# Layer 1's feed-forward scales the second projection's input instead of its output, and small weights are fetched a stage earlier

## What is computed

```python
x = x + tanh(g_xattn[l]) * attention_l(layernorm(x), ctx_1024, ...)
x = x + tanh(g_ffn[l])   * feed_forward_l(layernorm(x), ...)
```

```python
h = gelu(x @ w1[e]) * (x @ v1[e])            # for each expert e
out = sum_e gate[token, e] * (h @ w2[e]) + bias
```

## Time and profile before

| what | value |
|---|---|
| three timed executions | 1097.5, 1100.67, 1102.53 us, median 1100.67 |
| the profiled execution | 1095.08 us, of which the profile's span is 1093.3 us |
| mean granted clock of PE | 0.913 of full speed |
| busy share of the span | PE 80%, DVE 68%, ACT 52%, POOL 38% |
| set-up, then layer 0 (attention, feed-forward) | begin at 0, 16.68 and 118.91 us |
| layer 1 (attention, feed-forward) | begin at 181.65 and 423.34 us |
| layer 2 (attention, feed-forward) | begin at 702.27 and 813.53 us |
| layer 3 (attention, feed-forward) | begin at 873.81 and 1002.59 us |

### The profile page before, as it was taken

How to read it: one execution, slowest core, us unless ns; L and a number is a source line. 1 busy time by engine, 2 the same in 40 slices (tenths; PEclk the granted TensorE clock), 3 DMA queues, 4 the chain that set the end, 5 groups by cost and what they waited for, 6 DMA issues and landing times. The chain is left out here.

```text
span 1093.3 us, 17068 instructions
## 1 busy us (share of the span) xinstructions
PE 879.5 (80%) x5336; PEld 666.8 (61%) x5336; DVE 746.9 (68%) x1844; ACT 565.1 (52%) x1091; POOL 414.0 (38%) x559
## 2 busy tenths in 40 slices
PE   1899585789999994888888888489966668995795
PEld 0677463666666653666666666368854437995573
DVE  3699577589999984666757656468856514555786
ACT  1587263367777772545646454257743333432364
POOL 1543214133344431565656656444311042321143
PEclk9899688679999996999999999789988889998699
DMA  4000000000000001000000000000000020000001
GB/s 129 9 2 2 1 0 24 1 21 21 22 22 21 22 21 39 1 1 1 1 1 1 1 1 1 2 2 2 2 22 1 0 77 1 1 2 1 0 1 39
DMA packets 25926, 14.13 MB, mean 13 GB/s; under 512 B 11095, under 2 KB 25326, under 8 KB 25710
## 3 DMA queue, kind: packets, MB, share of 16 engines
q1 hardware_dynamic: 25838, 13.04, 4.4%
HBM read 11.99 MB, written 1.05 MB: 12 GB/s over the span
## 5 line engine op out<-in xcount | busy, mean ns | idle before, releaser
L1495 POOL TENSOR_TENSOR L1f_h<-L1f_h,L1f_gb 128x512 f32<-128x512 f32 (+1 forms) x96 | 152.2, 1588 | 104.6 <-DVE L1f_h L1788 96.2
L762 ACT ACTIVATE L_pt<-bank 128x512 f32<-128x512 f32 x224 | 127.0, 597 | 40.7 <-PE bank L637 26.6
L423 POOL TENSOR_TENSOR L_kc<-L_kc_all,const 128x256 fp32r<-128x256 f32 x96 | 58.8, 616 | 154.7 <-PE bank L637 73.6
L1624 ACT ACTIVATE L1f_a<-bank 128x512 f32<-128x512 f32 (+1 forms) x96 | 57.3, 596 | 111.8 <-PE bank L1549 111.8
L1788 DVE TENSOR_TENSOR L1f_h<-L1f_a,bank 128x512 f32<-128x512 f32 (+1 forms) x96 | 65.5, 682 | 70.2 <-ACT L1f_a L1624 69.6
L1796 DVE TENSOR_TENSOR L1f_h_lo<-L1f_h,L1f_h_hi 128x512 fp32r<-128x512 f32 (+1 forms) x96 | 88.0, 917 | 11.1 <-ACT L1f_h_hi L1637 11.1
L892 DVE TENSOR_REDUCE L_ms<-bank 128x2 f32<-128x512 f32 x128 | 83.6, 684 | 4.1 <-PE bank L595 3.5
L749 ACT ACTIVATE L_part<-bank,L_bias_ca,const 128x256 fp32r<-128x256 f32 x128 | 68.7, 562 | 29.5 <-PE bank L572 28.5
L1547 PE MATMUL bank<-L1f_xt_hi,big_hi 128*128 128x512 f32 (+1 forms) x192 | 77.5, 403 | 0.1
L1549 PE MATMUL bank<-L1f_xt_hi,big_lo 128*128 128x512 f32 (+1 forms) x192 | 76.5, 398 | 0.0
L1548 PE MATMUL bank<-L1f_xt_lo,big_hi 128*128 128x512 f32 (+1 forms) x192 | 76.3, 397 | 0.0
(11 more groups left out here) (410 smaller groups left out, 2505.0 us busy)
## 6 DMA issues: line engine op xcount, KB each, us to landing
L_raw<-in_L_ffn_w_dram SPq DMA_DIRECT2D x8, 176.0 KB, 2.3
L_raw<-in_L_ffn_v_dram SPq DMA_DIRECT2D x8, 176.0 KB, 2.5
const<-in_const_dram SPq DMA_DIRECT2D x1, 1036.0 KB
x<-in_x_dram SPq DMA_DIRECT2D x2, 512.0 KB
L_raw<-in_L_ffn_w_dram SPq DMA_DIRECT2D x8, 128.0 KB, 2.6
mask<-in_mask_Bx1xSxS_ff_dram SPq DMA_DIRECT2D x2, 512.0 KB
out_dram<-x SPq DMA_DIRECT2D x2, 512.0 KB
L_raw<-in_L_ffn_w_dram SPq DMA_DIRECT2D x8, 48.0 KB, 2.4
```

The lines of the kernel that those rows point to most:

```text
L762: act.activation(pt[:, g // 2, (g % 2) * NS + (HEADS_1[i] if own_keys else i)], b_st[(g * NS + i) % 2][:], ACT.Exp, scale=scale).then_inc( ...
L1495: pool.tensor_tensor(h[0:m, r], h[0:m, r], gb[0:m, gate_slot(c)], ALU.mult).then_inc(sem["h_done"], 1)
```

## The change

**Layer 1's feed-forward** is a function of its own, `ffn_gated_input`. Once per expert PE spreads the gates (`gate`), DVE multiplies the raw input by them into `xg_raw`, ACT casts `xg_hi`, POOL subtracts to `xg_lo` (both are `gated`), and the second projection (`u`) works on these. `up` is cut into `g` (first projection) and `u`, and `g` stands five chunks ahead of `u`; the tile `a` has 7 buffers instead of 4. POOL's multiplication of `h` and ACT's copy `gb` are gone; `split` follows one chunk behind. The front of the next batch stands at other chunks, its choice of experts in five parts over five chunks.

**Transfers**: the bias vectors of both attentions are issued in set-up, those of layer 0 ahead of the attention weights, those of layer 2 behind them. The integer weights of layer 2's feed-forward and the five loads of layer 3's attention are issued at the start of layer 2's attention. **Layer 2's feed-forward**: the three low parts are made behind the first scaling. **Layer 3's attention**: the eight value products leave the preparation and stand in the loop, one per sequence (`context_values`), through the bank that the transposes use.

```diff
+                def load_bias(layer):
+                    names = {0: ("L0_xattn_bq", "L0_xattn_bkv"), 2: ("L2_xattn_bq", "L2_xattn_bk")}[layer]
+                    for i, name in enumerate(names):
+                        for t in range(4):
+                            sp.dma_start(pr.bias_t[layer][NG * i:NG * i + NG].rearrange("g (h t d) -> g h t d", h=GH, t=4)[:, :, t],
+                                         ins[name][0:D].rearrange("(g h d) -> g h d", g=NG, h=GH)).then_inc(pr.bias_in[layer], 16)
+
+                load_bias(0)
...
+                load_bias(2)
...
-    ("values", 1), ("proj", 1, 1), ("pv", 0, 0), ("sums", 0), ("scores", 1, 0), ("scores", 1, 1), ("parts", 0), ("y", -1), ("keys", 2, 0),
+    ("context_values", 1), ("values", 1), ("proj", 1, 1), ("pv", 0, 0), ("sums", 0), ("scores", 1, 0), ("scores", 1, 1), ("parts", 0), ("y", -1), ("keys", 2, 0),
...
+                if layer == 2:
+                    for dst, src in ((pr.wi[:, 0:3], ins["L2_ffn_w_gate"].rearrange("(c p) d -> p c d", p=P)),
+                                     (pr.wi[:, 3:6], ins["L2_ffn_w_up"].rearrange("(c p) d -> p c d", p=P)),
+                                     (pr.wi[:, 6:9], ins["L2_ffn_w_down"].rearrange("d (c p) -> d c p", p=P))):
+                        sp.dma_start(dst, src).then_inc(pr.wi_in, 16)
+                    for dst, src in ((pr.w3[:, 1], ins["L3_xattn_Wk"]), (pr.w3[:, 0], ins["L3_xattn_Wq"]), (pr.w3[:, 2], ins["L3_xattn_Wv"]),
+                                     (pr.w3[:, 3].rearrange("p (c n) -> p c n", n=D), ins["L3_xattn_Wo"].rearrange("(c p) n -> p c n", p=P)),
+                                     (pr.bo3[:], ins["L3_xattn_bo"].partition_broadcast(P))):
+                        sp.dma_start(dst, src).then_inc(pr.w3_in, 16)
                 if layer == 0:
...
-                for e in range(B):
-                    bank = pr.bank[(NC + e) % 8]
-                    if e >= 4:
-                        pe.wait_ge(sem["prep_act"], e - 4 + 1)
-                    pe.matmul(bank[:], pr.ctx_t2[:, e].rearrange("p a s -> p (a s)"), wv[:], start=True, stop=True).then_inc(sem["prep_pe"], 1)
-                pe.wait_ge(sem["prep_act"], 12)
+                pe.wait_ge(sem["prep_act"], 4)
...
+                def context_values(b):
+                    pe.wait_ge(sem["xt_lo"], b + 1)
+                    pe.matmul(b_turn[:], pr.ctx_t2[:, b].rearrange("p a s -> p (a s)"), wv[:], start=True, stop=True).then_inc(sem["v_done"], 1)
...
+                def context_values(b):
+                    act.wait_ge(sem["v_done"], b + 1)
+                    act.copy(v_all[:, b], b_turn[:]).then_inc(sem["v_taken"], 1)
...
+                    if layer == 2 and i == 0:
+                        low_weights()
+
+                def low_weights():
+                    for m in range(3):
+                        cols = slice(m * 384, (m + 1) * 384)
+                        dve.wait_ge(sem["prep_act"], m + 1)
+                        prep(dve.tensor_tensor(lo[:, cols], pr.bank[m][:, 0:384], hi[:, cols].bitcast(F32), ALU.subtract))
 
...
+def ffn_gated_input(pr):
+    nc, ins = pr.nc, pr.ins
+    n = "L1f"
+    C, E, K = 24, E1, K1
+    N, NQ = NI * C, NI * E
+    AHEAD = 5
+    RA, R = 7, 4
+    LAG = 3
...
+            run(("moments", 0), ("prepare", 0), ("scale", 0), ("moments", 1), ("turn", 0), ("moments", 2), ("logits", 0))
+            run(*[("route", (0, part)) for part in range(5)])
+            run(("g", 0), ("g", 1), ("moments", 3), ("g", 2), ("gates", 0), ("g", 3), ("gate", 0), ("gated", 0), ("g", 4))
+            for k in range(N):
+                i, c = divmod(k, C)
+                if k + AHEAD < N:
+                    run(("g", k + AHEAD))
+                run(("u", k), ("mul", k))
+                if c % 3 == 0 and k // 3 + 1 < NQ:
+                    run(("gate", k // 3 + 1))
+                if c % 3 == 1 and k // 3 + 1 < NQ:
+                    run(("gated", k // 3 + 1))
+                if k >= 1:
+                    run(("split", k - 1))
+                if k >= LAG:
+                    run(("down", k - LAG))
+                if c == LAG - 1 and i:
+                    run(("y_copy", i - 1))
+                if i + 1 < NI:
+                    if c == 4:
+                        run(("scale", i + 1))
+                    if c == 6:
+                        run(("turn", i + 1))
+                    if c == 8:
+                        run(("logits", i + 1))
+                    if 9 <= c < 14:
+                        run(("route", (i + 1, c - 9)))
+                    if c == 15:
+                        run(("gates", i + 1))
+                if i and c == 11:
+                    run(("y_turn", i - 1))
+            run(("split", N - 1))
+            run(*[("down", k) for k in range(N - LAG, N)])
+            run(("y_copy", NI - 1), ("y_turn", NI - 1))
+
+        with nc.Block() as block:
+            @block.sync
+            def _(sp):
+                sp.dma_start(router[:], ins["L1_ffn_router_w"]).then_inc(sem["loaded"], 16)
...
+                def gated(q):
+                    pool.wait_ge(sem["xg_hi"], q + 1)
+                    need(pool, sem["u_done"], 3 * (q - 1))
+                    pool.tensor_tensor(xg_lo[:, q % 2], xg_raw[:, q % 2], xg_hi[:, q % 2].bitcast(F32), ALU.subtract).then_inc(sem["xg_lo"], 1)
...
+                def g(k):
+                    i = k // C
+                    pe.wait_ge(sem["xt_lo"], i + 1)
+                    need(pe, sem["act_done"], k - 1)
+                    product(b_g[k % 2], weights_at(k)[0], rows(k), xt_hi[:, i % 2], xt_lo[:, i % 2]).then_inc(sem["g_done"], 1)
+
+                def gate(q):
+                    i, e = divmod(q, E)
+                    pe.wait_ge(sem["gts_ready"], i + 1)
+                    need(pe, sem["xg_raw"], q - 1)
+                    pe.matmul(b_gate[q % 2][:], sel[:, e:e + 1].to_broadcast([P, P]), gts[:, i % 2], start=True, stop=True).then_inc(sem["gate_done"], 1)
+
+                def u(k):
+                    q = k // 3
+                    pe.wait_ge(sem["xg_lo"], q + 1)
+                    need(pe, sem["h_done"], k - 1)
+                    product(b_u[k % 2], weights_at(k)[1], rows(k), xg_hi[:, q % 2], xg_lo[:, q % 2]).then_inc(sem["u_done"], 1)
...
+                def g(k):
+                    m = rows(k)
+                    act.wait_ge(sem["g_done"], k + 1)
+                    need(act, sem["h_done"], k + 1 - RA)
+                    act.activation(a[0:m, k % RA], b_g[k % 2][0:m], ACT.Gelu).then_inc(sem["act_done"], 1)
+
+                def gated(q):
+                    act.wait_ge(sem["xg_raw"], q + 1)
+                    need(act, sem["u_done"], 3 * (q - 1))
+                    act.copy(xg_hi[:, q % 2], xg_raw[:, q % 2]).then_inc(sem["xg_hi"], 1)
+
...
+                def gate(q):
+                    dve.wait_ge(sem["xt_raw"], q // E + 1)
+                    dve.wait_ge(sem["gate_done"], q + 1)
+                    need(dve, sem["xg_lo"], q - 1)
+                    dve.tensor_tensor(xg_raw[:, q % 2], xt_raw[:, q // E % 2], b_gate[q % 2][:], ALU.mult).then_inc(sem["xg_raw"], 1)
+
+                def mul(k):
+                    m, r = rows(k), k % R
+                    dve.wait_ge(sem["act_done"], k + 1)
+                    dve.wait_ge(sem["u_done"], k + 1)
+                    need(dve, sem["lo_done"], k + 1 - R)
+                    dve.tensor_tensor(h[0:m, r], a[0:m, k % RA], b_u[k % 2][0:m], ALU.mult).then_inc(sem["h_done"], 1)
+
...
         with nc.sbuf_tensor("mask2", [P, NT, 2, S2], F32) as pr.mask2:
-            ffn(pr, 1)
-            attention(pr, 2, own_keys=False, masked=True, biased=True, scale=D ** -0.5)
-        ffn(pr, 2)
-        attention3(pr)
+            ffn_gated_input(pr)
+            with nc.sbuf_tensor("wi", [P, 9, P], I32) as pr.wi, nc.sbuf_tensor("w3", [P, 4, 512], F32) as pr.w3, \
+                    nc.sbuf_tensor("bo3", [P, D], F32) as pr.bo3:
+                attention(pr, 2, own_keys=False, masked=True, biased=True, scale=D ** -0.5)
+                ffn(pr, 2)
```

301 lines of the change are left out of this document (260 added, 41 removed).

## The result

The changed kernel takes 1048.5 us, the median of four runs (1046.1 to 1051.8), against 1100.9 us (1097.5 to 1102.5, four runs) for the kernel before: a ratio of 0.952, 95% interval 0.948 to 0.956. The forecast was 1046 us. In its profiled execution the span is 1048.7 us instead of 1093.3, with nearly the same mean clock of PE (0.916 against 0.913).

A forecast was written before the change was run, and what follows sets the result against it. The chain of `h` through POOL, not the matmuls, bounds layer 1's feed-forward. Terms -40.0 - 4.7 - 4.0 - 7.2 + 1.6 = -54.3 us give 1040.8 from the profiled 1095.08, 1046 from the 1100.67 median; range 1034 to 1070.

The forecast's parts named there:

- Layer 1's feed-forward: Layer 1's feed-forward: PE's matmuls alone remain, with 5 us allowed for all stops; 212.5 us from 252.52, -40.0 us.
- ring: Layer 1's feed-forward: making the gated input, gates' matmul through POOL's subtraction, takes 4.3 to 4.7 us against 5.8.
- the entry: Layer 1's feed-forward, before the first `down`: costs the same as before, within 2 us either way.
- Two signs: Layer 1's feed-forward, new profile: 6.5 to 6.7 us from expert to expert, and no PE wait for `h_lo`.
- The account of the stop: Layer 1's feed-forward, old kernel: PE loses 1.26 us per expert; `h_lo` is late as DVE's subtraction waits for POOL.
- Layer 2's attention: Entry of layer 2's attention: without the wait for bias vectors, token transposes start earlier; -4.7 us, between -3.5 and -5.
- feed-forward (-4.0; -4.0): Layer 2's feed-forward: DVE's 2.63 us wait for `wi` goes, first product comes earlier; -4.0 us, -3.6 to -4.2.
- Layer 3's attention: Layer 3's attention: early loads give -14.2 us, value products in the loop cost +7.0; -7.2 us, between -14 and 0.
- The entry (-14.2; -13.7): Layer 3's attention: first token transposes come 6.9 us after the block's start instead of 21.1, -14.2 us.
- stand several steps after the product: Layer 3's attention loop: POOL's `values` and PE's `y` await the value copy several steps after the product, 0.9 + 0.6 us.
- Set-up: Set-up: sixteen bias transfers keep SP issuing until 23.4, first attention begins near 24.0; +1.6 us, between +0.5 and +3.
- the slower case: Layer 1's feed-forward: PE's in-order wait for `xg_lo` blocks ready work, an expert takes 9.2 us; 1127 us, 3%.

The follow-up runs named there:

- gated_only: The kernel before with only layer 1's feed-forward replaced by the changed kernel's `ffn_gated_input`: 1065.6 us, ratio 0.968.
- att3_pieces: The changed kernel with POOL's 128x1920 subtraction in layer 3's attention cut into five of 128x384: 1042.1 us, ratio 0.949.
- best2: The changed kernel with layer 2's bias transfers and eight attention weights of layers 1 and 2 issued later, POOL's layer 3 subtraction in five pieces: 1034.7 us, ratio 0.940.
- pool_extra: The changed kernel with one more POOL multiplication of spare tiles per chunk of layer 1's feed-forward, its result unused: 1108.0 us, ratio 1.007.
- ahead0: The changed kernel with no `g` running ahead in layer 1's feed-forward, each directly before its own `u`: 1054.1 us, ratio 0.952.

## Why the prediction was right, step by step

- **Layer 1's feed-forward (-40.0; -39.9, and -40.2 in `gated_only`).** Right in mechanism and size. Expert 6.46 us, ring 4.29 us against 4.3 to 4.7, 1.47 us to spare against 1.1, stops of a few us. Inside the sum two terms missed and nearly cancelled: the stretch behind the first `down` was 210.0 instead of 212.5 us, and the entry 24.6 instead of 21.8 us, outside the 2 us that I had allowed. Both have one main reason: I let 26 matmuls stand ahead of the first `down`, but with `g` five ahead there are 42, and 16 by 0.231 is 3.7 us. Two signs came out only in part: experts beside a batch's front took up to 7.8 us, not 6.7, and PE still waited three times for `h_lo`, 0.6 us in all. The account of the stop was right in its chain and one-sided in its cause: I read the collision of the earlier trace rows as what made `h_lo` late, but the collisions are as many as before and cost nothing now; the chain was too long for its lag. So the gates' place was not the only cure: the new order with one more chunk of lag gives 32 of the 40 us.
- **Layer 2's attention (-4.7; -4.9) and feed-forward (-4.0; -4.0).** Right. The waits were the bound, and what stood next was where the rows put it. In twelve executions with these parts the two blocks took 160.8 to 165.4 us, in two without them 171.3 and 171.5. How the 4.0 us of the feed-forward divide between the early load and the later low parts was not tested.
- **Layer 3's attention (-7.2; -3.7 in that execution).** The entry (-14.2; -13.7) and the iteration (+0.88; +0.85) were right. The step that failed was the sentence that the waits for the value copy "stand several steps after the product". In the first iteration POOL's product for the values now waits 2.5 us for it, and its cast and subtraction of the next block's weights, which stand behind, come to lie on DVE's copy: a stop of 4.01 us instead of 2.05, and 7.6 us at a mean clock of 0.55 instead of 0.78. `att3_pieces` shows that the stop is a cause (117.85 us against 123.0 to 125.1 in nine profiles with the uncut instruction); how much of the lost clock follows from it stays open, since `best2` with the same pieces took 121.71. That the block's size was still as forecast on the mean is in part luck: 123.9 us over nine executions with the unaltered changed code, 131.0 over two of before, -7.1.
- **Set-up (+1.6; +2.4, over ten executions with this set-up +1.9 to +3.6).** The mechanism was right (SP's queue sets the end; begin 24.36 against 24.0), the size low: the wait for the weights' spreading ended at 25.81, not 25.4, and behind it DVE reached `xn` 2.0 us later than before.
- **The untouched blocks.** The forecast had no term for them, and they moved: +4.3 and +1.6 us. `gated_only` shows that layer 1's attention moves by more than that with nothing ahead of it changed.
- **The whole.** Sum in the profile -44.6 instead of -54.3 us; the timed medians -52.3. The difference of 9.7 is +4.3 and +1.6 of the untouched blocks, 3.5 of layer 3's attention and 0.8 of set-up, less 0.5 of the rest. The forecast misses by 2 us in the medians and by 9.7 in the profiles, because the profiled execution of before lies 5.8 us under its median and that of after 1.9 us above. That 1046 lies so near 1048.5 is therefore partly luck: single executions of one kernel differ by more.

The rivals: the slower case did not come, and nothing in the changed kernel is near it. But `pool_extra` took the time to 1108 us largely by its mechanism, the wait for `xg_lo` ahead of ready work (34.5 of the 52 us), with one POOL instruction per chunk: the ring's 1.47 us to spare is a small margin in the design.

## What to carry to other kernels

Where one engine's list is full and in order, ask of each chain beside it how many us of its work stand between the chain's start and its use, and compare that with the chain's length; move or shorten only the chain that is longer. A long elementwise instruction on POOL held up two kinds of DVE work here until it ended, copies and subtractions with both inputs in on-chip memory: keep it off the path, or cut it into pieces. Transfers issued ahead cost their issue time on SP's queue where they are issued, so put them into a block in which SP is idle, and count what they were covering.

## What was not expected of the hardware

- The same code at the same place of the program took 241.6 to 252.5 us (layer 1's attention, fourteen executions), by where and how long PE's clock was at half (mean 0.897 to 0.838), with PE's busy share at 86 to 88% in all. One profile of each kernel can't tell 5 us in such a block; a block with a full PE repeats to 0.5 us.
- 96 POOL instructions of 1.56 us, for whose results nobody waits, add 33 us to DVE's busy time and 17.4 us to a block in which DVE was at 79%.
- A copy of 128x32 took 3.2 to 3.6 us instead of 0.18 beside one POOL instruction of 4.23 us in eight of nine profiles (1.47 in `ahead0`, where it began later), and 0.38 and 0.91 beside pieces of about 1.0.
